# First attention of a two-layer block: the causal mask moves from TensorE to GpSimd, and VectorE's side work is dealt out anew

## The reference

```python
w1, w2 = jnp.split(w, 2, axis=-2)
w1 = _rmsnorm_noscale(w1)          # mean square over heads, to the power -1/2
logits = jnp.einsum('bnth,bnsh->bnts', q, k)
logits = _cross_head_proj(logits, pre_qw1, pre_qw2, pre_kw1, pre_kw2, pre_qdd, pre_kdd)
logits = jnp.where(mask, logits, jnp.finfo(jnp.float32).min)
probs = jax.nn.softmax(logits, axis=-1)
probs = _cross_head_proj(probs, post_qw1, post_qw2, post_kw1, post_kw2, post_qdd, post_kdd)
o = jnp.einsum('bnts,bnsh->bnth', probs, v)
```

## Time and profile before

| | us |
|---|---|
| median of 3 runs | 1052.75 (1050.74 to 1054.9) |
| the profiled execution: its time, its span | 1053.66, 1051.9 |
| PE busy, DVE busy, ACT busy, POOL busy | 910.1, 791.7, 573.7, 189.0 |
| the attention of layer 0, first to last `first_rank` | 50.1 to 421.6 |
| mean granted TensorE clock | 0.948 of full |

### The profile page before, as it was taken

One profiled execution on the slowest core, in us unless ns is written; L12 is line 12 of the kernel. 1 busy time (PEld: TensorE's weight loads), 2 busy tenths in 40 slices (PEclk: granted clock), 3 DMA queues, 4 the chain that ended last, 5 costly groups with the idle time before them and its releaser, 6 DMA issues.

```text
span 1051.9 us, 18274 instructions
## 1 busy us (share of the span) xinstructions
PE 910.1 (87%) x6216; PEld 654.6 (62%) x6216; DVE 791.7 (75%) x2089; ACT 573.7 (55%) x1458; POOL 189.0 (18%) x168
## 2 busy tenths in 40 slices
PE   2889888998899889689999999788888997899993
PEld 1677776777777777554566666523333437688883
DVE  7589988998899889984299996557666765466564
ACT  2698478857785788341233332146574761455551
POOL 1102030203020302047244433100000005011211
PEclk9999998999899989879999999969999988799998
DMA  9999950000000000034477884424464544787863
GB/s 248 199 210 234 242 136 1 1 1 2 1 1 2 1 1 1 1 133 174 128 225 225 253 246 132 162 80 160 165 236 160 206 174 160 256 323 293 287 259 131
DMA packets 71454, 153.81 MB, mean 146 GB/s; under 512 B 11440, under 2 KB 53055, under 8 KB 67137
## 3 DMA queue, kind: packets, MB, share of 16 engines
q1 hardware_dynamic: 65696, 139.93, 44.4%
q0 software_dynamic: 5664, 12.71, 3.3%
HBM read 122.09 MB, written 62.19 MB: 175 GB/s over the span
## 4 chain that ended last, share of the span: by engine, by line
PE 50%; DVE 27%; ACT 7%; DMA 7%; issue 5%; POOL 3%; SPq 1%; DVEq 0%; ACTq 0%; POOLq 0%
PE ps L1785 46%; DVE arena L1535 2%; DVE den L1033 2%; DVE arena L1217 2%; DVE arena L1191 2%; DMA arena<-split 2%; DMA made<-arena 2%; DMA arena<-slots 2%; POOL slots L580 1%; DVE arena L1200 1%; DVE arena L1174 1%; POOL arena L542 1%; ACT arena L693 1%; DVE arena L1764 1%; ACT arena L686 1%
## 5 line engine op out<-in xcount | busy, mean ns | idle before, releaser
L1785 PE MATMUL ps<-arena 128*128 128x128 f32 (+15 forms) x4652 | 708.1, 331 | 35.3 <-DVE arena L1191 14.8
L1785 PEld LDWEIGHTS ps<-arena 128*128 128x128 f32 (+7 forms) x4652 | 488.1, 149 | 182.1 <-issue 84.2
L1535 DVE TENSOR_REDUCE arena<-ps 128x4 f16<-128x1024 f32 (+1 forms) x48 | 58.9, 1228 | 53.5 <-PE ps L1785 53.5
L1217 DVE SCALAR_TENSOR_TENSOR arena<-arena 128x128 f32<-128x128 f32 x240 | 92.2, 447 | 0.5
L1762 DVE CAST arena<-arena 128x128 f16<-128x128 f32 (+1 forms) x128 | 33.2, 260 | 63.1 <-ACT arena L912 60.5
L657 ACT ACTIVATE arena<-ident,arena 128x128 f32<-128x128 f32 x256 | 80.2, 390 | 0.0
L817 ACT ACTIVATE arena<-ps 128x1024 f32<-128x1024 f32 x48 | 49.2, 1024 | 47.6 <-PE ps L1785 47.6
L912 ACT ACTIVATE arena<-ps,arena 128x128 f32<-128x128 f32 (+1 forms) x128 | 50.0, 416 | 44.2 <-PE ps L1785 39.2
L560 POOL DMA_INDIRECT made<-arena x47 | 53.0, 1128 | 87.2 <-DVE arena L1448 86.7
L1191 DVE SCALAR_TENSOR_TENSOR arena<-arena,ps 128x128 f32<-128x128 f32 (+1 forms) x128 | 47.0, 409 | 23.9 <-PE ps L1785 20.5
L528 POOL TENSOR_TENSOR den<-den,backd 128x512 f32<-128x512 f32 x8 | 10.5, 1313 | 270.2 <-DVE euv L1014 270.2
(11 more groups left out here) (301 smaller groups left out, 1232.2 us busy)
## 6 DMA issues: line engine op xcount, KB each, us to landing
arena<-split SPq DMA_DIRECT2D x15, 2048.0 KB, 9.5
arena<-in_w0all SPq DMA_DIRECT2D x32, 608.0 KB, 4.7
slots<-in_blank SPq DMA_DIRECT2D x17, 1040.0 KB, 18.8
arena<-in_w1all SPq DMA_DIRECT2D x16, 1024.0 KB, 6.8
split<-arena SPq DMA_DIRECT2D x32, 512.0 KB, 3.1
slots<-in_blank SPq DMA_DIRECT2D x10, 1044.0 KB, 23.0
arena<-slots SPq DMA_DIRECT2D x47, 130.0 KB, 3.1
side<-made SPq DMA_DIRECT2D x8, 512.0 KB, 6.3
```

Of the source, the lines that this page charges most:

```text
L1217: ins = dve.scalar_tensor_tensor(dst, prob[:, n % 3, tiles[tt]], w, dst, ALU.mult, ALU.add)
L1535: dve.tensor_reduce(out, ps[:, at:at + 2].rearrange("p j (r s) -> p j r s", r=nr), X, ALU.max, negate=True).then_inc(max1_done, 1)
L1785: return pe.matmul(o, l, r, start=start, stop=stop, skip_group_check=shared)
```

## The change

Four things are changed, all in the first attention.

1. The two `causal` products a round leave PE. Instead POOL writes the constant -1e30 into the two diagonal blocks of `second` with `affine_select` (128 partitions by 2x128 elements, one instruction a head, 64 in all), after ACT's `second_rank(n)` and ahead of DVE's `maximum(n)`, which now waits for it (`second_masked`). `first_rank` no longer waits for `second_rank`.
2. POOL's sums stand between these: of slice 2b (b over 0) behind the select of head 3, of slice 2b+1 behind that of head 15 (13 in batch 0).
3. The factor of the normalisation goes on `w2` instead of `w1`, so that DVE can form `qw` and `kw` (L1144, L1146) ahead of its wait for POOL's power.
4. DVE's side steps are dealt anew. In batches 1 to 3 rounds 0 and 1 have none; steps 6 to 11 of slice 2b follow rounds 2 and 3, the scans of slice 2b+1 rounds 4 to 6, `own_term` round 6. Scans of slice 2b+2 move within the batch's front and end by one place. ACT's first round normalises ahead of the next second ranks, and one of its copies (`rankkT[:, 1]`) stands behind two second ranks.

```diff
@@ -540,8 +541,15 @@
             for b in range(B):
                 pool.wait_ge(norm_in, b + 1)
                 pool.tensor_tensor(ms, ms, spread(small[:, 40:42], 1, TT * 4), ALU.pow).then_inc(norm_out, 1)
-                for n in range(2 * b if b else 1, 2 * b + 2):
-                    sum_slice(n)
+                for n in range(N0):
+                    pool.wait_ge(second_ready, b * N0 + n + 1)
+                    diagonal = second[:, n % 2].rearrange("p (a s) -> p a s", a=3)[:, 0::2]
+                    pool.affine_select(diagonal, diagonal, [[0, 2], [-1, P]], ALU.is_ge, MASKED, base=0,
+                                       channel_multiplier=1).then_inc(second_masked, 1)
+                    if b and n == 3:
+                        sum_slice(2 * b)
+                    if n == (15 if b else 13):
+                        sum_slice(2 * b + 1)
             sum_slice(2 * B)
 
             pool.wait_ge(blank0, 16 * (E0 + 1))
@@ -663,8 +671,6 @@
                     diagonals_pre(n)
                 act.wait_ge(projected, b * PROJ0 + 19)
                 act.activation(rankq[:, 1], ps[:, 3, 0:384], ACT.Copy).then_inc(evac_a, 1)
-                act.wait_ge(projected, b * PROJ0 + 21)
-                act.activation(rankkT[:, 1], ps[:, 5, 0:384], ACT.Copy).then_inc(evac_a, 1)
 
                 def exps(n):
                     s = n % 2
@@ -703,6 +709,8 @@
                 act.wait_ge(evac_a, b * EVA0 + 17)
                 second_rank(0)
                 second_rank(1)
+                act.wait_ge(projected, b * PROJ0 + 21)
+                act.activation(rankkT[:, 1], ps[:, 5, 0:384], ACT.Copy).then_inc(evac_a, 1)
                 for p in range(N0 // 2 + 1):
                     pair = (2 * p, 2 * p + 1)
                     if p:
@@ -713,15 +721,20 @@
                     for n in pair:
                         if n < N0:
                             exps(n)
+                    if p == 0:
+                        normalise(0)
+                        normalise(1)
                     for n in pair:
                         if n + 2 < N0:
                             second_rank(n + 2)
+                    if p == 0:
+                        diagonals_pre(4)
                     for n in pair:
-                        if n < N0:
+                        if p and n < N0:
                             normalise(n)
                             if n % 2 == 0 and n + 4 < N0:
                                 diagonals_pre(n + 4)
-                    if p == 1:
+                    if p == (4 if b else 1):
                         exp_slice(2 * b + 1)
 
                 exp_slice(2 * b + 2)
@@ -1128,17 +1141,13 @@
                 st(dve.tensor_reduce(ms, sq, X, ALU.add))
                 st.settle()
                 st.tell(dve.tensor_scalar(ms, ms, 1.0 / N0, 1e-6, ALU.mult, ALU.add), norm_in, b + 1)
-                for step in split[3:4]:
+                for step in split[2:3]:
                     step()
                 scaled_qk(1, 3)
                 st.settle()
                 stack_heads(1)
                 if b:
                     residual_first(b - 1)
-                dve.wait_ge(norm_out, b + 1)
-                st.tell(dve.tensor_tensor(flat[:, :, 0:2], flat[:, :, 0:2], spread(ms, 3, N0), ALU.mult),
-                        mix_ready, b + 1)
-                st.settle()
                 for tt in range(TT):
                     q, k = heads(qk[:, tt, 0]), heads(qk[:, tt, 1])
                     st(dve.tensor_tensor(qw[:, tt].rearrange("p i (n h) -> p i n h", h=HD0), spread(q, 1, 2),
@@ -1146,6 +1155,9 @@
                     st.tell(dve.tensor_tensor(kw[:, tt].rearrange("p i (n h) -> p i n h", h=HD0), spread(k, 1, 2),
                                               spread(mixw[:, tt, 1, 0:2], 3, HD0), ALU.mult),
                             stacked, b * 4 + tt + 3)
+                dve.wait_ge(norm_out, b + 1)
+                st.tell(dve.tensor_tensor(flat[:, :, 2:4], flat[:, :, 2:4], spread(ms, 3, N0), ALU.mult),
+                        mix_ready, b + 1)
                 for at, u in enumerate(TURNED_DVE):
                     dve.wait_ge(projected, b * PROJ0 + 8 + u)
                     st.tell(dve.tensor_copy(turned(u), turned_bank(u)), evac_d, b * EVD0 + 4 + at)
@@ -1155,14 +1167,13 @@
                         st.tell(ins, values_ready, b + 1)
                     else:
                         st(ins)
+                dve.wait_ge(mix_ready, b + 1)
                 for i, part in enumerate((fold, fold_tmp)):
                     st(dve.tensor_tensor(part, spread(mixw[:, :, 3, i], 3, N0), spread(mixw[:, :, 3, 2 + i], 2, N0), ALU.mult))
                 dve.wait_ge(projected, b * PROJ0 + 18)
                 st.tell(dve.tensor_copy(rankq[:, 0], ps[:, 2, 0:384]), evac_d, b * EVD0 + 6)
                 st.settle()
                 st(dve.tensor_tensor(fold, fold, fold_tmp, ALU.add))
-                for step in split[4:6]:
-                    step()
                 st.settle()
                 own_head = fold.rearrange("p t m n -> p t (m n)")[:, :, 0::N0 + 1]
                 st(dve.tensor_tensor(own_head, own_head, dd[:, :, 48:64], ALU.add))
@@ -1175,8 +1186,12 @@
                                       v0.rearrange("p t (n h) -> p t n h", h=HD0), spread(fold[:, :, n], 3, HD0),
                                       ALU.mult).then_inc(folded_ready, 1)
 
+                for step in split[3:4]:
+                    step()
                 dve.wait_ge(projected, b * PROJ0 + 20)
                 st.tell(dve.tensor_copy(rankkT[:, 0], ps[:, 4, 0:384]), evac_d, b * EVD0 + 7)
+                for step in split[4:6]:
+                    step()
                 st.settle()
                 tiles = (slice(0, P), slice(P, 384))
 
@@ -1184,7 +1199,6 @@
 
                     s = n % 2
                     dve.wait_ge(s_ready, b * N0 + n + 1)
-                    dve.wait_ge(second_ready, b * N0 + n + 1)
                     if n >= 2:
                         dve.wait_ge(p_exp, b * N0 + n - 1)
                     for tt in range(TT):
@@ -1196,6 +1210,7 @@
                 def maximum(n):
 
                     s = n % 2
+                    dve.wait_ge(second_masked, b * N0 + n + 1)
                     for tt in range(TT):
                         ins = dve.tensor_tensor_reduce(logit[:, s, tiles[tt]], logit[:, s, tiles[tt]],
                                                        second[:, s, tiles[tt]], -1.0, 3.0e38, ALU.add, ALU.min,
@@ -1223,8 +1238,12 @@
 
 
                 own, following = slice_steps(2 * b + 1, 2 * b + 1), slice_steps(2 * b + 2, 2 * b + 2)
-                extra = {0: split[6:12] + own[0:1], 1: own[1:2], 2: own[2:3], 3: own[3:4], 4: own[4:5], 5: own[5:6],
-                         7: own[6:9] + following[0:1]}
+                if b:
+                    extra = {2: split[6:9], 3: split[9:12] + own[0:1], 4: own[1:3], 5: own[3:4],
+                             6: own[4:6], 7: own[6:8] + following[0:1]}
+                else:
+                    extra = {0: own[0:1], 1: own[1:2], 2: own[2:3], 3: own[3:4], 4: own[4:5], 5: own[5:6],
+                             7: own[6:9] + following[0:1]}
                 for p in range(N0 // 2 + 1):
                     if p < N0 // 2:
                         first_rank(2 * p)
@@ -1258,7 +1277,7 @@
                     if p == 3 and 0 < b < B - 1:
                         condition_batch(b + 1, 0, b + 2)
 
-                late_own = own[9:12] if b else []
+                late_own = own[8:12] if b else []
                 for step in late_own[0:1]:
                     step()
                 for i in range(2):
@@ -1274,8 +1293,6 @@
                 st.settle()
                 flat_o = o_tok.rearrange("p t c -> p (t c)")
                 st.tell(dve.tensor_tensor(flat_o, flat_o, ps[:, 6], ALU.add), tail_dve, b * TAILD0 + 3)
-                for step in following[2:3]:
-                    step()
                 dve.wait_ge(tail_pe, b * TAIL0 + 4)
                 for i in range(2):
                     st(dve.tensor_tensor(o_tmp[:, i].rearrange("p t (n h) -> p t n h", h=HD0),
@@ -1288,7 +1305,7 @@
                 split = following
                 if b == B - 1:
                     condition_rows(1, slice(0, DONE0), 1, 1)
-                    for step in split[3:6]:
+                    for step in split[2:6]:
                         step()
 
             own_term_bounded(0)
@@ -1866,9 +1883,6 @@
                             rows, g = slice(32 * (n % 4), 32 * (n % 4) + 32), n // 4
                             mm(ps[:, n % 2, cols], qsT[rows, g, tt * P:(tt + 1) * P], ksT[rows, g, 0:(tt + 1) * P],
                                tt == 0, False, True)
-                    for n in pair:
-                        mm(ps[:, n % 2, 0:384].rearrange("p (a j) -> p a j", a=3)[:, 0::2], identb[:],
-                           spread(causal[:], 1, 2), False, False, True)
 
                 pe.wait_ge(evac_a, b * EVA0 + 13)
                 scores(0)
```

1 line of the change is left out of this document (added).

## The result

| | us |
|---|---|
| the changed kernel, median of 4 runs | 1067.58 (1062.44 to 1067.93) |
| the kernel before beside it, median | 1052.07 |
| ratio, 95% interval | 1.0137 [1.0106, 1.0167] |
| forecast | 1051.5, range 1041 to 1061 |
| its profiled execution: time, span | 1067.93, 1066.1 |

The account below looks back on a forecast made before the run. DVE and PE were both taken as full in steady rounds, with PE starved in the first rounds of three batches. Terms of -11.9 + 9.3 - 1.8 - 1.0 - 1.3 - 1.3 + 6.8 = -1.2 us gave 1051.5, range 1041 to 1061.

Parts of the forecast that it names:

- A: Rounds 0 and 1 of batches 1 to 3: steps leave, slice 2b's sums come in; 16.0 us after, -11.9 us.
- B: Moved steps reappear behind rounds 2 to 6, partly covered by DVE's idle time: +3.1 us net a batch, +9.3 us.
- G: The 64 selects on POOL: 34 counted as holding DVE 0.2 us each, +6.8 us, between 0 and 18.7.
- D: With F, the mask's products off PE: -1.0 us at the fronts, -1.3 in batch 0's rounds, 0 in the others.
- E: Batch ends: a scan ahead of DVE's last product moves behind the norm's signal; 3 x 0.44, -1.3 us.
- C: Batch 0's front: DVE's wait for the power now stands behind `qw` and `kw`; -1.8 us, hidden in other batches.
- F: With D, the mask's products off PE: -1.0 us at the fronts, -1.3 in batch 0's rounds, 0 in the others.
- Rival 3: PE's clock falls elsewhere, in rounds 3 and 4, behind waits of some 2 us; 7.7 us back, 1059; chance 0.06.

Follow-up runs that it names:

- e6: The changed kernel with POOL's four additions of slices 2, 4 and 6 left out; 1056.52 us, ratio 1.0028.
- e3: As e1, but DVE's steps dealt as in the kernel before, with slice 2b+1's sums behind head 13; 1050.6 us, ratio 0.9977.
- e1: The changed kernel with slice 2b's sums behind the select of head 1 instead of head 3; 1060.77 us, ratio 1.0079.
- e10: The changed kernel with slice 2b's six steps back in round 0, its sums behind head 1, slice 2b+1's steps still late; 1066.82 us, ratio 1.0122.
- e9: The changed kernel with slice 2b's steps still late, slice 2b+1's a round or two earlier, its sums behind head 13; 1063.06 us, ratio 1.0089.
- e7_power_alone: The kernel before with only DVE's wait for the power moved behind `qw` and `kw`; 1046.8 us, ratio 0.9933.
- e4: The kernel before with the new front only: power's result on `w2`, scans in their new places; 1051.47 us, ratio 0.9992.
- e2: The kernel before with the mask on POOL and sums between the selects, its steps and front unchanged; 1059.53 us, ratio 1.006.
- e7_early_scans: As e3, but slice 2b's scans, own term and sums where the kernel before has them, sums ahead of the first select; 1048.65 us, ratio 0.9956.
- e5: The changed kernel with 41 products that nothing reads where PE waits, in batches 1 to 3; 1061.46 us, ratio 1.0081.
- e11: e7_early_scans with 44 products that nothing reads ahead of `scores(2)` in batches 1 to 3; 1041.32 us, ratio 0.9889.

## Why the prediction was wrong

**A, rounds 0 and 1: right in size.** 15.88 us against 16.0. How long the sums hold DVE was wrong all the same: 4.0 us (e6), where the forecast had 2.9 and let 2.0 of it show. The mix was put at 2.0 and took 2.05; the fold was put at 0.5 and was not held; the maximum was put at 0.4 and took 2.1. It reads two tensors from SBUF as the fold does, and it is the instruction that ACT waits for. Of the 4.0 us 2.1 show as length there, and it did not end there: round 2 got, where the forecast had nothing, ACT's wait of 2.42 us, PE's of 1.99 and 1.31, and the lower clock. e6 prices the sums in this place at 8 us over three batches by the routing, where the forecast had 6. The Trainium skill, "SBUF — State Buffer", section "Who interferes with whom", says that an instruction of VectorE with two SBUF inputs contends with a GpSimd instruction that reads SBUF, and that `tensor_scalar` can contend too when its operands meet certain conditions; the rows of the additions agree (1.35 and 1.48 us against 0.28 and 0.41; 3.19 against 1.14). The forecast had quoted the first of this for the selects and gave the maximum only 0.4.

**B, where the steps go: the step that failed.** It said +3.1 us a batch net: 5.6 us of moved steps, less 2.45 us of DVE's idle time that they would fill. The rounds in which they land got longer by 7.1, 6.9 and 5.2 us (rounds 2 to 6), and what lies behind them by 2.5, 2.5 and 6.1. Over three batches that is 30.3 us, where the forecast had 9.3 in B, 4.8 in G and -1.4 in D and E, 12.7 in all. DVE's waits in these stretches, which were to fall by 7.4 us, rose from 14.4 to 23.9; it was to be busy for over 97% of rounds 2 to 7, and was for 91% of rounds 2 to 6 of batch 1 (44.42 of 48.94 us).

The pair e3 and e1, alike but for the deal, isolates it. Rounds 0 and 1 get 12.1 us shorter (65.2 to 53.1), although 18.3 us of busy time leave them (all over three batches); all behind them gets 23.8 us longer (241.2 to 264.9). Of the 23.8, 17.5 are busy time, and 6.3 are new waits where the forecast had 7.4 of cover. The error was to add up the idle time of a stretch (1.4 and 1.05 us) and to let the moved steps fill it. Cover belongs to the single round. Round 2 lasts 8.06 us by PE, and its one scan is hidden beside that (e10 against e3). Taking it out frees nothing there, and a second one in round 4 is paid nearly in full, with a slower clock in the round behind it. Both halves of the deal have the scans of slice 2b+1 begin behind round 4, which fits with each half costing nearly the whole; no run tries that alone. The cover at the batch's end was also counted once too often: in batch 3 of the kernel before DVE does not wait there (its copy L1266 at 432.72 follows at once).

What made the ends longer is not the reciprocal that moved there. The sums of slice 2b+1 now stand beside round 7 and hold a fold, a maximum and a mix for 3.1 us in each batch. In batch 3 PE then waits for ACT, and DVE for PE. DVE, then PE:

```profile
432.48 3.41 DVE L1232 SCALAR_TENSOR_TENSOR arena<-arena 128x128 f32<-128x128 f32 x4
...
446.81 1.02 DVE L1285 COPY arena<-ps 128x384 f32<-128x384 f32 x2 [2.89 <-PE ps L1968]
```

```profile
438.20 1.60 PE L1919 MATMUL ps<-ident,arena 128*128 128x128 f32 x6 [4.77 <-ACT arena L699]
```

The 3.1 us and the wait of 2.89 are the 6.1 of that end. Yet e9, which has these sums in round 6 again, pays as much in rounds 2 to 6 (157.6 us over three batches against 144.2) as it gains at the ends (115.1 against 129.5), so the forecast's 0 for this move, taken by itself, is not refuted.

**C, the power in batch 0: right.** -1.8 forecast, -2.1 measured (50.09 to 47.98), and e7_power_alone shows the later wait as the only part of the change that gains by itself. **E, the batch ends: not seen.** What e4 gained there (1.1 us a batch: 42.24 to 41.14) it lost again in round 0, for the later own term made the sums late, and they held the first maximum. The forecast followed the scans past PE's wait and not past POOL's sums. In the changed kernel, whose sums of slice 2b stand behind head 3, the ends carry the other slice's sums instead.

**G, the selects: oversized.** The forecast gave them 6.8 us. They are longer than thought, 0.75 us each in the mean (0.40 at the shortest), yet rounds 2 to 6 with them take 41.99 to 42.02 us against 41.81 (e2, e3, e7_early_scans). DVE's busy time grows by 1.05 us in those rounds of batch 1 (e3: 41.49 against 40.44) for some ten selects, and most of that falls into waits. As a length that is 0.2 us in these rounds, where the forecast had 1.6 a batch. By the rule that the prediction quotes each select that it counts would have cost its whole length; the fold at 164.06 (below) shows one that cost nothing.

**D and F, the mask off PE: not a gain on the whole.** In e3 rounds 2 and 4 of batch 1 are 0.33 us shorter than before (8.39 to 8.06, 8.24 to 7.91), and rounds 3 and 6 longer (8.42 to 8.81, 9.35 to 9.90); rounds 2 to 6 together gain nothing (41.81 to 42.00).

**The rivals.** Rival 3, given 0.06, came true in part: the clock falls in another place. Its place was right (round 4 has the wait of 2.17 us, round 3 none of that size), and so was its sign. Against it stood that the waits are far apart, and that was no protection: the clock is 0.50 at 189.7, behind waits of PE of 0.66 and 2.17 us. That its price of 7.7 us is the clock's share of the 15 us is not shown. Two things came with it that no rival had: round 2, starved by the sums, and waits that one hidden step a round had covered.

**What stays open.** How the 15 us split into load and clock is not settled. e5 shows 1.74 us of clock in one round, but since the fall moves when it is filled, no run here had the new deal at full clock throughout. No run puts the new deal alone on the kernel before, with its mask on PE and its sums ahead of the rounds; e1 against e3 shows its price only with the sums behind head 1. And why the clock fell in batch 1 of e11 and not in its other batches was not tried.

## What to carry to other kernels

Price a moved step by the round it lands in, not by the idle time of the stretch: one hidden step a round can be free and the second cost its full length, and a round that loses its hidden step need not get shorter. When a helper engine can hold up the bottleneck, look at which instruction stands beside it. The same four additions cost next to nothing ahead of the rounds, 1.7 us a batch when their end met the first maximum, and 4.0 us of busy time a batch (8 us of time over three batches) beside a mix and a maximum in round 1. Look also whether a wait that you blame is in the trace at all: here it was an instruction that took longer. And read a long program at a landmark behind the change: whole spans wandered by 7 us where nothing was changed, the landmark by 1 to 2.

## What was not expected of the hardware

- POOL's additions of 128x512 f32 (1.26 to 1.39 us each) held a `tensor_scalar` of DVE with a single SBUF input (1.14 to 3.19 us for four), and the custom maximum with two (0.28 to 1.35).
- `affine_select` on 128x256 f32 took 0.40 us at the shortest and 0.75 in the mean. One in the changed kernel took 1.01 us from 163.99 on, beside DVE's fold (from 164.06) and `first_rank` (from 164.66), which kept their 0.68 and 0.72 us. The pair of scans in a round took 1.42 us with selects about (e3, 165.52) and 1.27 without. Here it is POOL that gets longer, hardly DVE.
- The granted clock was 0.50 from 189.7 to 192.6 us in the changed kernel, behind two waits of PE, of 0.66 us and of 2.17 us that ended at 187.96. In e11 44 bf16 products of 0.11 us each (4.97 us) in place of an idle 5.36 us kept it at 1.00 and took 2.3 us off the 44 products behind them.
